# Two expert layers and a linear attention in one program: the iterations that only one stream fills get their router steps, row transposes and key product at other places

## The chip, the cores and the metric

One core of a Trainium2 chip runs the whole program. TensorE (PE) multiplies into PSUM, VectorE (DVE), ScalarE (ACT) and GpSimd (POOL) do the element-wise work, and SyncE (SP) issues most of the DMAs. Each engine works its own instruction list in order and waits on semaphores. The metric is the device time of one execution in microseconds; lower is better.

## The reference

For x of 32 sequences of 256 tokens with 128 channels:

```
x = x + 0.5 * ffn(layernorm(x), router, w1, w2)
x = x + attn(layernorm(x), W_qkv, W_out)
x = x + 0.5 * ffn(layernorm(x), router, w1, w2)

ffn:  probs = sigmoid(x @ router.T)            # 8 experts
      topw, sel = top_k(probs, 2);  topw = topw / (topw.sum + 1e-20)
      h = square(relu(x @ W1[e]))              # expert widths 4 x 128, 4 x 256
      out = sum over e of combine[e] * (h @ W2[e])
attn: q, k, v = x @ W_qkv, 16 heads of 8;  rope on q and k
      qf = elu(q * scale) + 1;  kf = elu(k) + 1
      out = (qf @ (kf.T @ v)) / max(qf . sum(kf), 1e-6);  out @ W_out
```

Every token goes through all eight experts and is weighted by its combine weight, which is zero for six of them. All of it is float32.

## The kernel before, in words

**Groups and streams.** The tokens are worked in NG = 16 groups of 512 tokens. Each group passes three stages: the first expert layer (stream f1), the attention (at), the second expert layer (f2). A software pipeline of 25 iterations (t from -3 to 21) runs f1, at and f2 of different groups side by side; f2 runs SHIFT = 5 groups behind f1. So only f1 has expert work in the first full iterations (t = -1 to 3) and only f2 in the last ones: these are the lone iterations, for which `alone(s, t)` holds.

**Chunks and places.** An expert layer is NC = 12 chunks of 128 hidden columns. An iteration has 24 places; where both streams run there is a chunk at each place, f1's in the first 12, f2's in the next 12; in a lone iteration the chunks stand at every second place. f2's twelve lone chunks begin at place 12 and end in the next iteration. One chunk is: three matmuls up (`up`, lines 509 to 511, the float32 product split in three fp32r products), relu times the gate on VectorE into `hid` (`weighted`, line 1047), the square and the rounded copy `h_hi` on ScalarE (`squares`, lines 740 and 751: the copy of a chunk is issued after the square of the next one of its group), the remainder `h_lo` on GpSimd (`remainders`, line 880), and nine places later three matmuls down (`down`, lines 529 to 531). `hid` has six slots and the up product two PSUM banks.

**The router and the gates.** For the group one iteration ahead: normalise (`norm`), transpose on TensorE (`transpose`, line 471), copy to `xT`, router product (`logits`, line 490), exp and 1 + exp on ScalarE (lines 718 and 722), then on VectorE `take_sigmoid` (972), `best_two` (981), `where_two` (990 to 995), `weigh_two` (1003 and 1007, gives cwt), `choose_two` (1015); on GpSimd `root_of_weights` (874, the square root of cwt, since the gate is applied before the square); on VectorE `spread_roots` (pick at 1025, g_tok at 1031). `weight_rows` transposes g_tok on TensorE (480), `rows_of_weights` copies the rows to SBUF on ScalarE (730), and SyncE writes them to DRAM (395) and broadcasts them to all 128 partitions in four DMAs of 512 KB and less (`g_all`, 407). Chunk 0 of the next group cannot be weighted before its piece of g_all has landed, and a piece is only overwritten when the group before has used it.

**What sets the order.** Each engine has one hand-written function `iteration(t, par)`; the place of a call in it is the place of the work in that engine's queue. TensorE writes transposes and logits into one PSUM bank (`tp`), and `tp_free` holds the order of its five users.

**The start.** w1 is split into `w1_hi` (ScalarE, line 822) and `w1_lo` (VectorE, line 922) in iteration -3, before the first logits; `keep_busy` (line 589) runs idle transposes on TensorE.

## Time and profile before

| | us |
|---|---|
| median of three runs (791.9 to 795.37) | 792.01 |
| the profiled execution | 793.06 |
| its span | 791.3 |

| engine | busy us | share |
|---|---|---|
| TensorE | 729.2 | 92% |
| GpSimd | 686.2 | 87% |
| ScalarE | 597.5 | 76% |
| VectorE | 581.6 | 74% |

Busy time is the sum over an engine's instructions; it doesn't say which engine the others wait for. The matmuls' ends are modelled, so that TensorE's share is no measure of its speed. What an engine waits for stands in the table of waits, and how long one iteration of the pipeline takes is the distance between two first chunks in the timeline. Of the 1.7 us between span and time of the profiled execution the profile shows nothing.

### The profile page before, as it was taken

What the parts mean: (1) busy time and instruction counts of PE and PEld (TensorE: products, weight loads), DVE (VectorE), ACT (ScalarE), POOL (GpSimd) and SP (SyncE); (2) the same over time, 40 slices, a digit from 0 to 9 for tenths busy, and PEclk for the clock granted to TensorE, in tenths of its full rate; (3) what the DMA queues carried; (4) which work ended last, traced back from release to release, by engine and by line L of the source; (5) the groups of instructions that cost most, each with busy time, mean ns of one, the idle gap of its engine ahead of it and who ended that gap; (6) DMA issues with size and microseconds to landing.
All of it is one profiled execution on the core that took longest, in us unless ns stands there. A gap on an engine that the chain in (4) does not pass through costs nothing.

```text
span 791.3 us, 13302 instructions
## 1 busy us (share of the span) xinstructions
PE 729.2 (92%) x3736; PEld 594.3 (75%) x3736; DVE 581.6 (74%) x1832; ACT 597.5 (76%) x1220; POOL 686.2 (87%) x668
## 2 busy tenths in 40 slices
PE   6688788889999999999999999999999998989887
PEld 6466566667888888888888888888887877767665
DVE  3456788877879787877878797878777678676543
ACT  4577677668887978888888879788878766766765
POOL 3778867859999999999999999999999877666876
PEclk9999999989999999999999999999999999999999
DMA  5654113023233222233333332213333403303330
GB/s 181 187 163 133 37 72 107 2 107 108 108 109 121 91 91 69 99 110 108 121 109 120 109 122 84 79 68 112 116 108 121 122 2 107 110 13 121 121 121 27
DMA packets 31160, 79.38 MB, mean 100 GB/s; under 512 B 3312, under 2 KB 14448, under 8 KB 31088
## 3 DMA queue, kind: packets, MB, share of 16 engines
q1 hardware_dynamic: 30800, 78.47, 29.9%
q8 instruction: 30, 0.49, 0.3%
q14 instruction: 42, 0.34, 0.1%
q10 hardware_dynamic: 288, 0.07, 0.0%
HBM read 73.81 MB, written 4.72 MB: 99 GB/s over the span
## 4 chain that ended last, share of the span: by engine, by line
PE 27%; DVE 27%; POOL 18%; issue 13%; ACT 10%; DMA 4%; DVEq 1%; POOLq 0%; ACTq 0%; SPq 0%
POOL h_lo L880 9%; DVE hid L1047 7%; POOL root_f L874 4%; PE bank L509 4%; PE bank L529 3%; PE bank L511 3%; PE bank L510 3%; PE bank L531 3%; PE bank L530 3%; DMA g_all_f<-rows_f 3%; ACT h_hi L751 3%; DVE pick_f L1025 2%; ACT hid L740 2%; POOL x_lo_at L868 2%; ACT xn_f L697 2%
## 5 line engine op out<-in xcount | busy, mean ns | idle before, releaser
L880 POOL TENSOR_TENSOR h_lo<-hid,h_hi 128x512 fp32r<-128x512 f32 x384 | 492.8, 1308 | 70.0 <-ACT h_hi L751 69.4
L1047 DVE SCALAR_TENSOR_TENSOR hid<-bank,g_all_f 128x512 f32<-128x512 f32 x384 | 262.2, 684 | 137.8 <-PE bank L511 90.9
L740 ACT ACTIVATE hid<-hid 128x512 f32<-128x512 f32 x384 | 228.8, 622 | 50.0 <-DVE hid L1047 49.7
L751 ACT ACTIVATE h_hi<-hid 128x512 fp32r<-128x512 f32 x384 | 225.8, 620 | 4.9 <-PE bank L531 0.4
L509 PE MATMUL bank<-x_hi_f,w_hi 128*128 128x512 f32 x384 | 164.3, 428 | 16.1 <-DVE hid L1047 16.1
L529 PE MATMUL bank<-h_hi,w_hi 128*128 128x512 f32 x384 | 154.5, 402 | 12.5 <-POOL h_lo L880 12.5
L531 PE MATMUL bank<-h_hi,w_lo 128*128 128x512 f32 x384 | 152.6, 397 | 0.0
L511 PE MATMUL bank<-x_hi_f,w_lo 128*128 128x512 f32 x384 | 151.9, 396 | 0.0
L530 PE MATMUL bank<-h_lo,w_hi 128*128 128x512 f32 x384 | 151.9, 396 | 0.0
L510 PE MATMUL bank<-x_lo_f,w_hi 128*128 128x512 f32 x384 | 151.5, 395 | 0.0
L509 PEld LDWEIGHTS bank<-x_hi_f,w_hi 128*128 128x128 f32 x384 | 73.1, 190 | 40.7 <-DVE hid L1047 25.2
L529 PEld LDWEIGHTS bank<-h_hi,w_hi 128*128 128x128 f32 x384 | 72.5, 189 | 34.9 <-POOL h_lo L880 20.0
L511 PEld LDWEIGHTS bank<-x_hi_f,w_lo 128*128 128x128 f32 x384 | 72.6, 189 | 17.6
L531 PEld LDWEIGHTS bank<-h_hi,w_lo 128*128 128x128 f32 x384 | 72.4, 188 | 16.6
L530 PEld LDWEIGHTS bank<-h_lo,w_hi 128*128 128x128 f32 x384 | 72.5, 189 | 15.4
L510 PEld LDWEIGHTS bank<-x_lo_f,w_hi 128*128 128x128 f32 x384 | 73.3, 191 | 11.1
L697 ACT ACTIVATE xn_f<-x_sb,nbias_f,rstd_f 128x128 f32<-128x128 f32 x128 | 52.4, 481 | 12.5 <-POOL nbias_f L861 12.5
L874 POOL TENSOR_TENSOR root_f<-cwt_f,c_half 128x8 f32<-128x8 f32 x32 | 54.3, 1697 | 0.0
L868 POOL TENSOR_TENSOR x_lo_f<-xT,x_hi_f 128x512 fp32r<-128x512 f32 x32 | 41.5, 1298 | 12.9 <-DVE x_hi_f L965 12.9
L709 ACT ACTIVATE xT<-bank 128x512 f32<-128x512 f32 x48 | 28.3, 590 | 26.4 <-PE bank L471 16.7
L965 DVE CAST x_hi_f<-xT 128x512 fp32r<-128x512 f32 x32 | 21.6, 676 | 24.3 <-ACT xT L709 24.3
L718 ACT ACTIVATE ex_f<-bank 128x32 f32<-128x32 f32 x32 | 6.3, 197 | 43.0 <-PE bank L490 43.0
(105 smaller groups left out, 1045.2 us busy)
## 6 DMA issues: line engine op xcount, KB each, us to landing
g_all_f<-rows_f SPq DMA_DIRECT2D x128, 512.0 KB, 5.8
x_sb<-in_x SPq DMA_DIRECT2D x16, 256.0 KB, 3.3
out_x<-x_sb SPq DMA_DIRECT2D x16, 256.0 KB, 7.1
g_all_f<-in_w SPq DMA_DIRECT2D x2, 768.0 KB, 6.6
con<-in_const SPq DMA_DIRECT2D x1, 584.0 KB, 6.1
rows_f<-g_row_f SPq DMA_DIRECT2D x32, 16.0 KB, 1.4
g_all_f<-in_wqkv SPq DMA_DIRECT2D x1, 192.0 KB, 6.5
con<-in_const ACTq DMA_DIRECT2D x1, 68.0 KB, 3.2
```

Of the source, the lines that this page charges most:

```text
L509: mm(o, w1_hi[:, w], x_hi[s][u][:], start=True, stop=False)
L510: mm(o, w1_hi[:, w], x_lo[s][u][:], start=False, stop=False)
L511: mm(o, w1_lo[:, w], x_hi[s][u][:], start=False, stop=True).then_inc(s_p1[s], 1)
L529: mm(o, w2_hi[:, c, :], h_hi[:, c, :], start=(c == 0), stop=False)
L530: mm(o, w2_hi[:, c, :], h_lo[:, c, :], start=False, stop=False)
L531: i = mm(o, w2_lo[:, c, :], h_hi[:, c, :], start=False, stop=(c == NC - 1))
L697: i = fn(xn[s][:, k, :], tile, ACT.Identity, bias=nbias[s][:, k:k + 1], scale=rstd[s][:, k:k + 1])
L740: fn(h, h, ACT.Square).then_inc(s_sq[s], 1)
L751: fn(h_hi[:, c, :], hid[:, c % STAGE, :], ACT.Copy).then_inc(s_hhi[s], 1)
L874: gp.tensor_tensor(root[s][:], cwt[s][:], c_half[:], ALU.pow).then_inc(s_root[s], 1)
L880: gp.tensor_tensor(h_lo[:, c, :], hid[:, c % STAGE, :], h_hi[:, c, :].bitcast(F32), ALU.subtract).then_inc(s_hlo[s], 1)
L1047: v.scalar_tensor_tensor(hid[:, c % STAGE, :], hp[c % 2][:], 0.0, g_all[s][:, EXPERT[c], :], ALU.max, ALU.mult).then_inc(s_z[s], 1)
```

## The change

Nothing is computed otherwise and no instruction is added, except in the start: the idle transposes are 27 and 24 where they were 36 and 16. All moves hold in lone iterations alone. In the first stream's, VectorE does `best_two` right after the sigmoid, `where_two` ahead of the fourth chunk, `weigh_two` and `choose_two` behind it and `spread_roots` behind the sixth; GpSimd takes the root one chunk earlier; TensorE transposes the weight rows at place 12 (it was 18), and ScalarE copies them there. In the second stream's, the router steps are drawn together in the same way, the attention's residual sum goes to place 15, TensorE makes keys and values at place 18 (it was 21), rope of the keys goes to places 19 and 20, and in the iteration behind TensorE and ScalarE make the rows at place 3 (it was 6), with `q_features` ahead of `k_features`. The split of w1 goes behind the first gates.

```diff
@@ TensorE
-            keep_busy(a2, 36)
+            keep_busy(a2, 27)
...
                 quarter(t, 0, par)
+                if alone("f2", t - 1):
+                    weight_rows("f2", t + 1 - SHIFT, t)
                 state(t - 2)
                 logits("f1", t + 2)
...
                 if first_time(True, t + 1):
-                    keep_busy(a2, 16)
+                    keep_busy(a2, 24)
                 quarter(t, 1, par)
-                weight_rows("f2", t + 1 - SHIFT, t, 1)
+                if not alone("f2", t - 1):
+                    weight_rows("f2", t + 1 - SHIFT, t)
...
                 if alone("f1", t - 1):
                     back("f1", t)
+                if alone("f1", t):
+                    weight_rows("f1", t + 2, t)
...
                 quarter(t, 5, par)
-                weight_rows("f1", t + 2, t, 4)
+                if not alone("f1", t):
+                    weight_rows("f1", t + 2, t)
+                if alone("f2", t):
+                    kv(t - 1, 0)
+                    kv(t - 1, 1)
                 quarter(t, 6, par)
-                kv(t - 1, 0)
-                kv(t - 1, 1)
+                if not alone("f2", t):
+                    kv(t - 1, 0)
+                    kv(t - 1, 1)
@@ ScalarE
                 exp_logits("f1", t + 2)
+                if first_time(True, t + 2):
+                    act.wait_ge(s_w1, 16)
+                    fn(w1_hi[:], w1_raw, ACT.Copy).then_inc(s_w1hi, 1)
                 squares(t, 0)
+                if alone("f2", t - 1):
+                    rows_of_weights("f2", n2)
...
                 copy_attnT(t - 2)
+                if alone("f1", t):
+                    rows_of_weights("f1", t + 2)
@@ GpSimd
-                remainders(t, 2, 3, 4, 5, 6)
-                root_of_weights("f1", t + 2)
+                remainders(t, 2, 3, 4)
+                if alone("f1", t):
+                    root_of_weights("f1", t + 2)
+                remainders(t, 5, 6)
+                if not alone("f1", t):
+                    root_of_weights("f1", t + 2)
```

`tp_free` now takes the name of the user and puts f1's rows ahead of f2's transpose where f1 is alone. VectorE's moves are shown by its rows. In them `hid` is a chunk's weighting, and f1 and f2 (f10, f20 with a buffer's number) the stream.

VectorE, second full iteration of the first stream (t = 0), from the second chunk's statistics on, before:

```order
L1047 SCALAR_TENSOR_TENSOR hid<-bank1,g_all_f1 128x512
L972 RECIPROCAL prob_f1<-odds_f1 128x32
L957 BN_AGGR mv_f1<-bn_f1 128x2 x4
L981 MAX best_f1<-prob_f1 128x8 x4
L1047 SCALAR_TENSOR_TENSOR hid<-bank2,g_all_f1 128x512
...
L1007 TENSOR_SCALAR cwt_f1,cw_sum_f1<-cw_f1 128x8
L1047 SCALAR_TENSOR_TENSOR hid<-bank2,g_all_f1 128x512
L1015 TENSOR_TENSOR chosen_f1<-which_f1,con 128x64
L1047 SCALAR_TENSOR_TENSOR hid<-bank1,g_all_f1 128x512
L1025 TENSOR_TENSOR pick_f1<-chosen_f1,root_f1 128x64
```

and now:

```order
L1072 SCALAR_TENSOR_TENSOR hid<-bank1,g_all_f1 128x512
L997 RECIPROCAL prob_f1<-odds_f1 128x32
L1006 MAX best_f1<-prob_f1 128x8 x4
...
L1072 SCALAR_TENSOR_TENSOR hid<-bank2,g_all_f1 128x512
L1028 TENSOR_TENSOR cw_f1<-best_f1,rtot_f1 128x8
L1032 TENSOR_SCALAR cwt_f1,cw_sum_f1<-cw_f1 128x8
L1040 TENSOR_TENSOR chosen_f1<-which_f1,con 128x64
L1072 SCALAR_TENSOR_TENSOR hid<-bank1,g_all_f1 128x512
L1072 SCALAR_TENSOR_TENSOR hid<-bank2,g_all_f1 128x512
L1050 TENSOR_TENSOR pick_f1<-chosen_f1,root_f1 128x64
```

The weights (cwt) stand behind the fourth chunk instead of the fifth, and the pick behind the sixth instead of the seventh.

TensorE in the same iteration, from the transpose back of the group before (L542) on, before:

```order
L542 MATMUL bank4<-con,yT 128x128 x4
L509 MATMUL bank1<-x_hi_f11,w1_hi 128x512
...
L509 MATMUL bank2<-x_hi_f11,w1_hi 128x512
...
L531 MATMUL bank3<-h_hi,w2_lo 128x512
L480 MATMUL bank0<-con,g_tok_f1 32x128
L509 MATMUL bank2<-x_hi_f11,w1_hi 128x512
```

and now:

```order
L547 MATMUL bank4<-con,yT 128x128 x4
L485 MATMUL bank0<-con,g_tok_f1 32x128
L514 MATMUL bank1<-x_hi_f11,w1_hi 128x512
L515 MATMUL bank1<-x_lo_f11,w1_hi 128x512
L516 MATMUL bank1<-x_hi_f11,w1_lo 128x512
```

The rows' transpose stands ahead of the up products of chunks 6, 7 and 8 instead of behind them, with three down products between: 18 matmuls in all.

VectorE in a lone iteration of the second stream (t = 18), before:

```order
L981 MAX best_f2<-prob_f2 128x8 x4
L1047 SCALAR_TENSOR_TENSOR hid<-bank2,g_all_f2 128x512
L990 TENSOR_REDUCE tot_f2<-best_f2 128x4
...
L1007 TENSOR_SCALAR cwt_f2,cw_sum_f2<-cw_f2 128x8
L1015 TENSOR_TENSOR chosen_f2<-which_f2,con 128x64
L1047 SCALAR_TENSOR_TENSOR hid<-bank2,g_all_f2 128x512
L1055 TENSOR_TENSOR x_sb<-bank3,x_sb 128x512
L1047 SCALAR_TENSOR_TENSOR hid<-bank1,g_all_f2 128x512
L1025 TENSOR_TENSOR pick_f2<-chosen_f2,root_f2 128x64
```

and now:

```order
L1006 MAX best_f2<-prob_f2 128x8 x4
L1015 TENSOR_REDUCE tot_f2<-best_f2 128x4
...
L1028 TENSOR_TENSOR cw_f2<-best_f2,rtot_f2 128x8
L1072 SCALAR_TENSOR_TENSOR hid<-bank2,g_all_f2 128x512
...
L1040 TENSOR_TENSOR chosen_f2<-which_f2,con 128x64
L1072 SCALAR_TENSOR_TENSOR hid<-bank1,g_all_f2 128x512
L1072 SCALAR_TENSOR_TENSOR hid<-bank2,g_all_f2 128x512
L1050 TENSOR_TENSOR pick_f2<-chosen_f2,root_f2 128x64
L1056 TENSOR_REDUCE g_tok_f2<-pick_f2 128x4x8
L1080 TENSOR_TENSOR x_sb<-bank3,x_sb 128x512
```

The router's steps move ahead of the chunks that stood between them, and the pick ahead of the residual sum and of chunk 6. GpSimd's root of f2 keeps its place, behind chunk 3's remainder.

## Rows read from the trace of the kernel before

**Rows 1.** The waits: engine and line, released by, us in total, times, longest.
```profile
DVE hid L1047 <- DMA g_all_f<-rows_f: 33.8, 10, 7.1
```

**Rows 2.** Busy time by window: length, PE, PEld, DVE, ACT, POOL, granted clock, DMA.
```profile
26.05:49.47 23.42, 19.04 (x79) 13.11 (x79) 12.56 (x42) 16.11 (x32) 19.46 (x18) 1.00 0.51 159
49.47:73.64 24.17, 20.03 (x88) 14.52 (x89) 14.08 (x51) 18.19 (x37) 19.97 (x22) 1.00 0.48 154
718.68:743.85 25.17, 22.14 (x99) 17.24 (x98) 13.65 (x44) 16.91 (x34) 19.01 (x18) 0.93 0.27 97
743.85:766.40 22.55, 19.97 (x89) 15.00 (x88) 13.51 (x35) 14.53 (x28) 19.38 (x16) 1.00 0.32 107
```

**Rows 3.** Timeline of VectorE, first chunks: start, us, line, [idle before, released by].
```profile
49.47 0.69 DVE L1047 SCALAR_TENSOR_TENSOR hid<-bank,g_all_f 128x512 f32<-128x512 f32 x1 [4.12 <-DMA g_all_f<-rows_f]
73.64 0.69 DVE L1047 SCALAR_TENSOR_TENSOR hid<-bank,g_all_f 128x512 f32<-128x512 f32 x1 [4.38 <-DMA g_all_f<-rows_f]
...
658.28 0.69 DVE L1047 SCALAR_TENSOR_TENSOR hid<-bank,g_all_f 128x512 f32<-128x512 f32 x1 [3.54 <-DMA g_all_f<-rows_f]
688.73 0.69 DVE L1047 SCALAR_TENSOR_TENSOR hid<-bank,g_all_f 128x512 f32<-128x512 f32 x1 [2.16 <-DMA g_all_f<-rows_f]
...
766.40 1.29 DVE L1047 SCALAR_TENSOR_TENSOR hid<-bank,g_all_f 128x512 f32<-128x512 f32 x2 [4.45 <-DMA g_all_f<-rows_f]
```

**Rows 4.** Timeline of the start, up to the first router steps.
```profile
4.01 6.13 PE L589 MATMUL bank<-con 128*128 128x128 f32 x36 [4.01 <-DMA con<-in_const]
7.59 1.65 ACT L697 ACTIVATE xn_f<-x_sb,nbias_f,rstd_f 128x128 f32<-128x128 f32 x4 [4.34 <-POOL nbias_f L861]
13.45 0.33 DVE L972 RECIPROCAL prob_f<-odds_f 128x32 f32<-128x32 f32 x1
```

**Rows 5.** Timeline of the iteration from 49.47 us: the gates' way.
```profile
59.14 1.29 POOL L880 TENSOR_TENSOR h_lo<-hid,h_hi 128x512 fp32r<-128x512 f32 x1 [1.34 <-ACT h_hi L751]
60.40 1.63 POOL L874 TENSOR_TENSOR root_f<-cwt_f,c_half 128x8 f32<-128x8 f32 x1
62.06 1.27 DVE L1025 TENSOR_TENSOR pick_f<-chosen_f,root_f 128x64 f32<-128x64 f32 x1 [2.36 <-POOL root_f L874]
64.10 0.27 PE L480 MATMUL bank<-con,g_tok_f 128*32 128x128 f32 x1
67.05 0.34 ACT L730 ACTIVATE g_row_f<-bank,c_cut 32x128 f32<-32x128 f32 x1
67.76 0.34 SPq L395 DMA_DIRECT2D rows_f<-g_row_f  x1
69.31 2.13 SPq L407 DMA_DIRECT2D g_all_f<-rows_f  x4
```

**Rows 6.** Timeline of TensorE there: a down and an up product.
```profile
65.05 0.40 PE L529 MATMUL bank<-h_hi,w_hi 128*128 128x512 f32 x1
65.75 0.39 PE L509 MATMUL bank<-x_hi_f,w_hi 128*128 128x512 f32 x1
```

**Rows 7.** Timeline, second stream: a pick in one iteration, the gates of the next.
```profile
731.73 0.23 DVE L1025 TENSOR_TENSOR pick_f<-chosen_f,root_f 128x64 f32<-128x64 f32 x1 [0.97 <-POOL root_f L874]
...
749.87 0.68 DVE L1047 SCALAR_TENSOR_TENSOR hid<-bank,g_all_f 128x512 f32<-128x512 f32 x1
751.81 1.29 POOL L880 TENSOR_TENSOR h_lo<-hid,h_hi 128x512 fp32r<-128x512 f32 x1 [0.64 <-ACT h_hi L751]
753.07 1.63 POOL L874 TENSOR_TENSOR root_f<-cwt_f,c_half 128x8 f32<-128x8 f32 x1
754.73 1.28 DVE L1025 TENSOR_TENSOR pick_f<-chosen_f,root_f 128x64 f32<-128x64 f32 x1 [1.60 <-POOL root_f L874]
759.74 0.34 ACT L730 ACTIVATE g_row_f<-bank,c_cut 32x128 f32<-32x128 f32 x1
```

**Rows 8.** Busy time by window, columns as in rows 2: two gaps of TensorE.
```profile
83.00:92.00 9.00, 5.53 (x25) 4.10 (x24) 5.63 (x10) 4.97 (x10) 7.96 (x7) 1.00 0.01 2
152.00:164.00 12.00, 8.41 (x36) 6.46 (x35) 11.54 (x49) 6.00 (x12) 8.35 (x11) 0.86 0.34 132
```

**Rows 9.** Timeline of TensorE: the gap inside the first window.
```profile
88.20 0.50 PE L556 MATMUL bank<-x_hi_at,wq_hi 128*128 128x512 f32 x1 [3.47 <-POOL x_lo_at L868]
```

More of the change, by code:

```diff
@@ L448, in _, with tp_free, transpose @@
             mm = nc.tensor.matmul
-            def tp_free(t, pos):
-                n = [done(m + (pos > k)) for k, m in
-                     enumerate((t + 2, t + 1 - SHIFT, t - 1, t + 2 - SHIFT, t + 2))]
-                if due(n[0]):
-                    pe.wait_ge(s_ex["f1"], value(n[0]))
-                if due(n[1]):
-                    pe.wait_ge(s_gr["f2"], value(n[1]))
-                if due(n[2]):
-                    pe.wait_ge(s_xT["at"], value(n[2]))
-                if due(n[3]):
-                    pe.wait_ge(s_ex["f2"], value(n[3]))
-                if due(n[4]):
-                    pe.wait_ge(s_gr["f1"], value(n[4]))
-            def transpose(s, n, t, pos):
+            def tp_free(t, user):
+                if alone("f1", t):
+                    order = ("f1", "f2 rows", "at", "f1 rows", "f2")
+                else:
+                    order = ("f1", "f2 rows", "at", "f2", "f1 rows")
+                pos = order.index(user)
+                group = {"f1": t + 2, "f2 rows": t + 1 - SHIFT, "at": t - 1, "f2": t + 2 - SHIFT, "f1 rows": t + 2}
+                n = {q: done(group[q] + (order.index(q) < pos)) for q in order}
+                if due(n["f1"]):
+                    pe.wait_ge(s_ex["f1"], value(n["f1"]))
+                if due(n["f2 rows"]):
+                    pe.wait_ge(s_gr["f2"], value(n["f2 rows"]))
+                if due(n["at"]):
+                    pe.wait_ge(s_xT["at"], value(n["at"]))
+                if due(n["f2"]):
+                    pe.wait_ge(s_ex["f2"], value(n["f2"]))
+                if due(n["f1 rows"]):
+                    pe.wait_ge(s_gr["f1"], value(n["f1 rows"]))
+            def transpose(s, n, t):
                 if not live(n):
@@ L478, in weight_rows @@
                 pe.wait_ge(s_gt[s], value(n + 1))
-                tp_free(t, pos)
+                tp_free(t, s + " rows")
                 nc.tensor.transpose(tp[0:EXP * TG, 0:P], g_tok[s][:].rearrange("p e k -> p (e k)"), ident) \
@@ L1158, in iteration @@
                     add_moe("f2", t - 1 - SHIFT)
-                k_features(t - 2)
-                q_features(t - 2)
+                if alone("f2", t - 1):
+                    q_features(t - 2)
+                    k_features(t - 2)
+                else:
+                    k_features(t - 2)
+                    q_features(t - 2)
                 weighted(t, 0)
                 high_part("f1", n1, par)
-                spread_roots("f2", n2_last, 0)
+                if not alone("f2", t - 1):
+                    spread_roots("f2", n2_last, 0)
                 weighted(t, 1)
-                spread_roots("f2", n2_last, 1)
+                if not alone("f2", t - 1):
+                    spread_roots("f2", n2_last, 1)
                 weighted(t, 2)
@@ L1189, in iteration @@
                 weighted(t, 10)
+                if alone("f1", t):
+                    spread_roots("f1", n1, 0)
+                    spread_roots("f1", n1, 1)
+                    if first_time(True, t + 2):
+                        split_w1()
                 high_part("at", t - 1, 0)
-                choose_two("f1", n1)
+                if not alone("f1", t):
+                    choose_two("f1", n1)
                 weighted(t, 11)
@@ L1209, in iteration @@
                 mean_variance("at", t)
[L1210 to L1213 removed]
+                if alone("f2", t):
+                    where_two("f2", n2)
+                    weigh_two("f2", n2, 0)
+                else:
+                    best_two("f2", n2)
+                weighted(t, 18)
+                if alone("f2", t):
+                    weigh_two("f2", n2, 1)
+                    choose_two("f2", n2)
+                    stats("f2", t + 3 - SHIFT, 0)
+                else:
+                    add_attention(t - 2)
+                    where_two("f2", n2)
                 weighted(t, 19)
                 rope_q_cos(t - 1)
[L1216 removed]
+                if alone("f2", t):
+                    rope_k(t - 1, 0)
+                else:
+                    weigh_two("f2", n2, 0)
                 weighted(t, 20)
                 rope_q_sum(t - 1)
[L1219 to L1220 removed]
+                if alone("f2", t):
+                    rope_k(t - 1, 1)
+                    rope_k_sum(t - 1)
+                    mean_variance("f2", t + 3 - SHIFT)
+                else:
+                    stats("f2", t + 3 - SHIFT, 0)
+                    weigh_two("f2", n2, 1)
                 weighted(t, 21)
[L1222 to L1224 removed]
+                if not alone("f2", t):
+                    mean_variance("f2", t + 3 - SHIFT)
+                    choose_two("f2", n2)
+                    rope_k(t - 1, 0)
                 weighted(t, 22)
[L1226 removed]
+                if alone("f2", t):
+                    spread_roots("f2", n2, 0)
+                    spread_roots("f2", n2, 1)
+                else:
+                    rope_k(t - 1, 1)
                 weighted(t, 23)
[L1228 removed]
+                if not alone("f2", t):
+                    rope_k_sum(t - 1)
             pipeline(dve, iteration)
```

63 lines of the change are left out of this document (34 added, 29 removed).

## The prediction, made before the changed kernel ran

> **What bounds the kernel now.** I read four views in this order. The table of waits comes first: VectorE stood 33.8 us in all for the gates' broadcast, ten times, once for 7.1 us [rows 1]. That is the most the change can go for: nearly all else it touches has cover. The timeline at the first chunks then says where these waits end something. A first chunk that starts straight behind such a wait sets the distance to the one before: in the first stream at 49.47 and 73.64 (4.12 and 4.38 us idle ahead of it), in the second at 658.28, 688.73 and 766.40 (3.54, 2.16, 4.45) [rows 3]. The busy times between two first chunks give the floor. GpSimd has 19.46 us of work in the 23.42 from 26.05 and 19.97 in the 24.17 from 49.47; in the tail 19.01 of 25.17 and 19.38 of 22.55 [rows 2]. TensorE in the second of them has 20.03, though its gaps are many. So if the gates came at once, a lone iteration would not fall to zero wait: GpSimd would stop it after 20 us, less than 4 us below now, plus whatever GpSimd itself idles. The middle of the program, where both streams run, keeps its order.
>
> Last, the way of the gates in the iteration from 49.47 [rows 5]: the root starts at 60.40, the pick at 62.06, TensorE transposes at 64.10, ScalarE copies the row only at 67.05, SyncE writes it at 67.76, broadcasts at 69.31, and it has landed at 73.64. From row copy to landing is 6.59 us, and nothing in the change shortens that. Between transpose and row copy lie 2.95 us of which the copy needs 0.34: the rest is ScalarE's queue (squares).
>
> **The start.** The 36 idle transposes take 6.13 us from 4.01 and end at 10.14; one is 0.17, so 27 end 1.5 us earlier, at 8.6. The normalised tokens are there at 7.59 + 1.65 = 9.24 [rows 4], so only 10.14 - 9.3, about 0.8, can be won. The split of w1 leaves VectorE's way to the sigmoid at 13.45 too, but the way there is TensorE's and ScalarE's; it is worth nothing more as long as w1's halves are ready for chunk 0, which waits 7.1 us for gates today [rows 1]. The eight more transposes in the next iteration cost 8 x 0.17 = 1.4 us of TensorE inside that wait. I take +0.75 (0 to 1.5).
>
> **First stream, 26.05 and 49.47.** The root moves one remainder (1.3 us) ahead. At 59.14 the remainder ahead of it had itself made GpSimd idle 1.34 us for ScalarE's copy [rows 5], so the root fits nearly into idle time, and g_tok comes about 2 us earlier. The rows' transpose now stands at place 12 instead of 18, ahead of chunks 6, 7 and 8. TensorE is in order, so it stands there until g_tok has come, an estimated 3 to 3.7 us after it is through with chunk 5, because GpSimd, not TensorE, paces those chunks. Behind the transpose it still has to do the products up to the next first chunk: six remaining up triples, the next chunk's one, and six down triples, 13 x 0.70 us (65.05 to 65.75 [rows 6]) = 9.1, plus 0.3 for the transpose and 0.5 for the first product's end: 9.9 us. g_tok is there 11.6 us behind the first chunk by my walk through the queues, so the next first chunk can come after 11.6 + 9.9 = 21.5. The gates would be there after 11.6 + 0.4 + 6.6 = 18.6: the wait for the broadcast goes, and TensorE's queue is late next. Against 23.42 that is +1.9. In the next iteration the GpSimd work is 0.5 us more and it idles while chunk 6 is behind the transpose: a remainder needs the copy that ScalarE issues behind the square of the next chunk, and that chunk is now queued behind the transpose. I put this idle time at 2.8 us, between the 1.34 that it waits at this place now [rows 5] and the 4.2 that would leave no gain: 19.97 + 2.8 = 22.8, against 24.17, +1.4. Bounds for the two together: -1 (GpSimd idle 4.5 us in each) to +6.5 (both at GpSimd's busy time plus 0.8).
>
> **First stream, the three later ones** (from 73.64). They don't end at a gate wait; VectorE has the attention's steps as well. There the moves save a part of VectorE's wait for the root (2.36 us ahead of the pick [rows 5]) and cost TensorE's new wait; I take a third of that wait once, +0.75, bounds -2 and +2.5. The second stream's transpose, which now waits for the row copy on the shared bank, lies in the last of them and is in these bounds.
>
> **Second stream.** Here the root keeps its place, behind chunk 3's remainder, and that remainder waits for ScalarE's copy (0.64 at 751.81 [rows 7]), which waits for chunk 4's square. The router steps (best, the sum, the four finds, reciprocal, weights, choose: about 2 us of short rows) now stand ahead of chunks 3 and 4, so root, today at 753.07, comes 0.8 to 1.7 us later. In exchange the pick is ahead of the residual sum, and the rows leave at place 3, not 6: from pick (754.73) to row copy (759.74) 5.0 us pass [rows 7], of which this can save some 3 where the attention fills the places between. I take +2.0 in the iteration that ends at 658.28 (of 3.54), -0.3 in the next, 0 at 718.68, +0.75 for the one to 743.85, where kv at place 18 gives the state earlier, and -1.3 for the last, where nothing but chunks lies between the places and only the late root is left. Sum +1.15; bounds -2 and +4. Half of the finds' cost would vanish if chunk 4's product is late anyway (TensorE gaps); that is in the bounds.
>
> **Sum.** 0.75 + 1.9 + 1.4 + 0.75 + 1.15 = 5.95, taken as 6.0. The profiled execution took 793.06 (span 791.3 and 1.7 around it), so 787.1; it stands 1.05 above the median of the three runs, 792.01, and against that I forecast 786.0.
>
> **Rivals.**
> *B, TensorE's clock.* In the window from 83 to 92, with a TensorE gap of 3.47 us [rows 9], the granted clock stayed 1.00; over 152 to 164 it was 0.86 [rows 8]. With 2.4 and 1.2 GHz as the levels, 0.86 over 12 us means 3.4 us at the lower one and 1.7 us of work lost. If the new stand at the transpose does this in two iterations in which TensorE's queue is late next, 3.4 us of the head's gain go: 6.0 - 3.4 = 2.6, 789.4. For it: the new gap is about as long as the longest. Against it: rows 8 show such a gap with the clock whole. The Trainium skill (TensorE: Matmul & The Clock Gate, section HAM oscillation) says that pauses of the matmul engine between bursts let its clock drop, so that the next burst starts slow each time; by it every lone iteration with the new stand would pay. This case's trace agrees in the one window and not in the other.
>
> *C, the second stream's late root costs more.* The tail's sum at its lower bound, -2, instead of +1.15: 789.1. For it: the root is behind a remainder that is already waited for (0.64). Against: the waits at 658.28 and 688.73 leave 2 to 3.5 us to win.
>
> *D, the slower side: GpSimd's loop.* Remainders of chunks 5 and 6 are held by the transpose, and GpSimd is the floor. If it idles more than 4.0 us from one first chunk to the next (23.42 - 19.46), the head gets longer. Price: 1.3 us, one remainder, in each of five lone iterations, 6.5, and the last tail term 1.3, less 0.75 from the start and 2.0 at 658.28: 5.0 us slower, 797. Against it: today's idle time at that remainder is 1.34 us [rows 5].
>
> *E, the moves do all they can.* TensorE's stand is under 2 us and the two iterations fall to about 20.5; with the tail at +3 the gain is 10: 782. Against it: 13 triples behind the transpose.
>
> **Chances.** Forecast 0.58 (its own range 783 to 789), B 0.16, C 0.12, D 0.09, E 0.05. What this kernel's measurement can tell from no change is 0.5%, 3.96 us: faster means under 788.05. The forecast's own range lies below that for 0.50 of its 0.58; E and a part of B and C give 0.10 more: faster 0.60. D is slower, 0.09; the rest, 0.31, is no change. The range takes in B and C and most of the forecast: 781.0 to 791.5. Nothing about the middle has to be allowed for.
>
> **What would show it.** Right: the waits for the broadcast fall from 33.8 to about 20; the distances in the first stream read near 21.5 and 22.8; TensorE stands 3 us or more ahead of the first stream's rows' transpose; ScalarE's row copy follows it within 0.5 us; the second stream's root starts 0.8 us or more later behind its first chunk. Wrong: a granted clock below 0.9 in the windows of the first lone iterations (B); GpSimd idle above 4 us there (D); a first chunk at 658.28 that still waits 3 us (C); or a middle part whose length changes, which no step here allows for.

## The result and the profile after

| | before | changed |
|---|---|---|
| median (seven runs each) | 791.9 us | 799.28 us (796.73 to 802.7) |
| profiled execution, its span | 793.06, 791.3 us | 802.7, 800.9 us |
| ratio of the times | | 1.0093, interval 1.0073 to 1.0113 |

The change made the kernel 0.9% slower; 786.0 us, 0.8% faster, had been forecast. The profiled execution of the changed kernel is one of its slower ones, 3.4 us above the median; the comparisons between kernels below go by medians, the traces tell where the time lies.

What the change aimed at, it reached. In the table of waits of the changed kernel (engine and line, released by, us in total, times, longest) the wait for the gates' broadcast is down from 33.8 us [rows 1] to 7.0:

```profile
DVE hid L1072 <- DMA g_all_f<-rows_f: 7.0, 4, 3.4
DVE pick_f L1050 <- POOL root_f L895: 21.3, 9, 3.6
PE bank L485 <- DVE g_tok_f L1056: 17.6, 10, 3.4
...
```

Two other waits grew in its place: VectorE stands for the root (12.4 us over 7 times before, 21.3 over 9 now) and TensorE for the weights that it is to transpose (1.7 us once before, 17.6 over 10 times now). VectorE's waits for a chunk's product rose too, from 90.9 to 104.4 us, and those for a slot that GpSimd has to free from 11.3 to 20.1.

Set beside the windows of before [rows 2], the same stretches of the changed kernel, each from one first chunk to the next (columns: length, PE, PEld, DVE, ACT, POOL, granted clock, DMA):

```profile
24.25:47.93 23.68, 18.65 (x84) 14.23 (x83) 12.58 (x42) 15.70 (x30) 17.04 (x17) 0.93 0.51 183
47.93:72.80 24.87, 20.77 (x90) 15.74 (x88) 14.68 (x51) 17.00 (x34) 19.85 (x22) 0.93 0.45 148
72.80:102.15 29.35, 24.83 (x114) 19.59 (x114) 21.65 (x63) 21.25 (x44) 24.89 (x25) 0.94 0.27 91
102.15:135.85 33.70, 28.81 (x136) 23.29 (x136) 25.75 (x81) 22.27 (x44) 24.35 (x27) 0.90 0.18 64
725.24:749.98 24.74, 21.84 (x99) 17.18 (x98) 14.45 (x44) 16.78 (x35) 18.91 (x19) 0.93 0.20 67
749.98:776.01 26.03, 22.16 (x93) 16.71 (x92) 13.26 (x36) 15.81 (x30) 20.32 (x16) 0.93 0.26 93
```

The third and fourth of before, which the rows above do not have:

```profile
73.64:101.25 27.61, 21.22 (x100) 16.01 (x98) 21.11 (x64) 18.82 (x38) 22.01 (x23) 1.00 0.29 100
101.25:131.73 30.48, 25.88 (x136) 20.62 (x136) 26.32 (x81) 22.03 (x44) 24.37 (x27) 1.00 0.25 83
```

The first chunk comes at 24.25 instead of 26.05 us, so 1.8 us are won in the start. From there on the first four distances read 23.68, 24.87, 29.35 and 33.70 (before: 23.42, 24.17, 27.61 and 30.48), and the last but one 26.03 where it was 22.55. Every one of these windows shows a granted clock under 1.00; the first four of before were at 1.00. GpSimd, which had the most work of the four in the first of them before (19.46 us), is idle for 6.6 of 23.68 us.

The way of the gates in the iteration from 47.93 (timeline: start, us, line, [idle before, released by]) beside [rows 5]:

```profile
58.05 1.64 POOL L895 TENSOR_TENSOR root_f<-cwt_f,c_half 128x8 f32<-128x8 f32 x1
59.72 1.28 DVE L1050 TENSOR_TENSOR pick_f<-chosen_f,root_f 128x64 f32<-128x64 f32 x1 [3.23 <-POOL root_f L895]
61.31 0.39 PE L485 MATMUL bank<-con,g_tok_f 128*32 128x128 f32 x1 [2.80 <-DVE g_tok_f L1056]
61.74 0.36 ACT L745 ACTIVATE g_row_f<-bank,c_cut 32x128 f32<-32x128 f32 x1 [0.62 <-PE bank L485]
...
67.25 2.56 POOL L901 TENSOR_TENSOR h_lo<-hid,h_hi 128x512 fp32r<-128x512 f32 x2 [3.86 <-ACT h_hi L766]
...
72.80 0.69 DVE L1072 SCALAR_TENSOR_TENSOR hid<-bank,g_all_f 128x512 f32<-128x512 f32 x1 [1.22 <-POOL h_lo L901]
```

Root, pick and transpose are at 10.1, 11.8 and 13.4 us behind the first chunk (49.47; before 10.9, 12.6, 14.6), the row copy at 13.8 instead of 17.6. TensorE stood 2.80 us for it, the remainder at 67.25 waited 3.86 us, and the next first chunk waits for no gate: it is released by GpSimd's remainder, through the six slots of `hid`.

The gap's other price, in windows around the stand of the iteration before (TensorE idle from 32.98 to 36.42), columns as above:

```profile
31.00:37.00 6.00, 1.76 (x8) 0.99 (x8) 2.40 (x4) 4.91 (x11) 6.00 (x5) 1.00 0.46 143
37.00:41.00 4.00, 4.00 (x12) 3.14 (x11) 1.38 (x2) 0.92 (x3) 1.50 (x2) 0.57 0.21 77
41.00:47.00 6.00, 6.00 (x30) 4.88 (x29) 2.77 (x4) 5.03 (x9) 4.21 (x4) 1.00 0.58 214
```

and single matmuls of it, in that stretch and behind it:

```profile
38.07 0.63 PE L536 MATMUL bank<-h_hi,w_lo 128*128 128x512 f32 x1
38.49 0.63 PE L514 MATMUL bank<-x_hi_f,w_hi 128*128 128x512 f32 x1
...
41.11 0.39 PE L515 MATMUL bank<-x_lo_f,w_hi 128*128 128x512 f32 x1
41.34 0.39 PE L516 MATMUL bank<-x_hi_f,w_lo 128*128 128x512 f32 x1
```

TensorE has hardly worked up to 36.4, and then runs at the lower of its two levels (1.2 instead of 2.4 GHz, 0.57 in the mean from 37 to 41): a matmul every 0.42 us instead of 0.23, just when six chunks' products are due. That is what the Trainium skill describes for waits on DMAs (TensorE: Matmul & The Clock Gate, section HAM oscillation: the engine waits, and its next burst begins cold, each time round); this trace agrees, with a wait on VectorE.

In the second stream, the iteration from 749.98, beside [rows 7]:

```profile
749.98 0.69 DVE L1072 SCALAR_TENSOR_TENSOR hid<-bank,g_all_f 128x512 f32<-128x512 f32 x1 [1.33 <-DMA g_all_f<-rows_f]
...
757.48 0.07 DVE L1032 DVE_READ_ACCUMULATOR cwt_f<-cw_f 128x1 f32 x1
...
760.04 1.30 POOL L901 TENSOR_TENSOR h_lo<-hid,h_hi 128x512 fp32r<-128x512 f32 x1 [1.94 <-ACT h_hi L766]
761.29 1.64 POOL L895 TENSOR_TENSOR root_f<-cwt_f,c_half 128x8 f32<-128x8 f32 x1
762.89 2.50 POOL L901 TENSOR_TENSOR h_lo<-hid,h_hi 128x512 fp32r<-128x512 f32 x2
762.97 1.27 DVE L1050 TENSOR_TENSOR pick_f<-chosen_f,root_f 128x64 f32<-128x64 f32 x1 [3.59 <-POOL root_f L895]
764.55 0.40 PE L485 MATMUL bank<-con,g_tok_f 128*32 128x128 f32 x1 [2.83 <-DVE g_tok_f L1056]
```

The root stands 11.3 us behind the first chunk; it was 9.2. The weights (cwt) were ready at 757.5. The root was not waiting for them but stood, in GpSimd's order, behind the remainder of chunk 3, and that remainder waited 1.94 us for ScalarE's copy, which comes behind chunk 4's square. VectorE then idled 3.59 us ahead of the pick with chunk 6 behind it.

### The profile page after: what moved, and what is told of

Same layout as the page of the kernel before. It is cut to its first block, busy times and chain, and to the rows that moved or that the text cites. A ratio compares the mean times of both kernels' runs of the same rounds, so it can differ in the third digit from the quotient of the medians.

```text
span 800.9 us, 13300 instructions
## 1 busy us (share of the span) xinstructions
PE 738.6 (92%) x3735; PEld 606.2 (76%) x3735; DVE 585.3 (73%) x1832; ACT 598.3 (75%) x1220; POOL 688.8 (86%) x668
## 4 chain that ended last, share of the span: by engine, by line
PE 34%; DVE 28%; POOL 16%; issue 12%; ACT 8%; DMA 1%; DVEq 1%; POOLq 0%; ACTq 0%; SPq 0%
POOL h_lo L901 8%; DVE hid L1072 7%; PE bank L514 4%; POOL root_f L895 4%; PE bank L516 4%; PE bank L515 4%; PE bank L534 4%; PE bank L536 4%; PE bank L535 4%; PE bank L495 2%; DVE pick_f L1050 2%; ACT h_hi L766 2%; PE bank L610 2%; POOL x_lo_at L889 2%; PE bank L622 2%
## 5 line engine op out<-in xcount | busy, mean ns | idle before, releaser
L1072 DVE SCALAR_TENSOR_TENSOR hid<-bank,g_all_f 128x512 f32<-128x512 f32 x384 | 262.2, 684 | 133.8 <-PE bank L516 104.4
L514 PE MATMUL bank<-x_hi_f,w_hi 128*128 128x512 f32 x384 | 165.4, 431 | 18.0 <-DVE hid L1072 17.6
L516 PE MATMUL bank<-x_hi_f,w_lo 128*128 128x512 f32 x384 | 153.9, 401 | 0.0
```

What stands on the lines that cost most here:

```text
L514: mm(o, w1_hi[:, w], x_hi[s][u][:], start=True, stop=False)
L516: mm(o, w1_lo[:, w], x_hi[s][u][:], start=False, stop=True).then_inc(s_p1[s], 1)
L1072: v.scalar_tensor_tensor(hid[:, c % STAGE, :], hp[c % 2][:], 0.0, g_all[s][:, EXPERT[c], :], ALU.max, ALU.mult).then_inc(s_z[s], 1)
```

## The experiments

Each was timed beside the kernel before on the same chip, and the median of that kernel lay between 791.75 and 792.56 us. "Start" below is the new start (27 and 24 idle transposes, w1 split behind the first gates). Diffs are against the changed kernel, where nothing else is said.

**Does the clock explain it?** Idle transposes fill the stand:

```diff
             def weight_rows(s, n, t):
...
+                tp_free(t, s + " rows")
+                if s == "f1" and alone("f1", t) and not isinstance(t, Step) and t in (-1, 0, 1, 2, 3,):
+                    keep_busy(tp, 12)
+                if s == "f2" and alone("f2", t - 1):
+                    keep_busy(tp, 12)
                 pe.wait_ge(s_gt[s], value(n + 1))
-                tp_free(t, s + " rows")
```

> The changed kernel with 12 idle transposes on TensorE (into the bank of the transposes, which is free by then) ahead of its wait for the weights to be transposed, in every lone iteration of both streams. Clock theory: the changed order lets TensorE stand in each lone iteration, the granted clock then falls to half for a stretch, and nine to ten such stretches of some 3.4 us cost about 1.7 us each. With the gap filled the clock goes back to 0.99 and the kernel to 787 to 791 us. Rival, order theory (remainders and products held behind the weights' transpose): the clock changes but the distances between first chunks do not, 799 us or, with 2 us more work on TensorE in ten iterations, up to 803.

Measured: 796.9 us (ratio 1.0054, 1.0031 to 1.0078), clock 0.991. The clock came back in all but one of the first lone iterations and only some 2.4 us with it. From first chunk to the start of the middle part the head fell from 148.1 to 143.9 us (before: 141.8), the tail from 140.2 to 139.5 (before: 133.0). That lies between the two theories. So the clock is part of the loss in the first stream; in the second, filling the stands gave back next to nothing, though the transposes take TensorE's time there too.

**The parts by themselves.** The kernel before with the start alone; then also the first stream's moves; then the second stream's moves alone. For each, the other stream's `if alone(...)` branches take the old side:

```diff
-                if alone("f2", t):
+                if False:
                     where_two("f2", n2)
```

> The kernel before with the new start alone (27 and 24 idle transposes, w1 split behind the first gates). In the changed kernel the first chunk came at 24.25 us instead of 26.05. Both theories: 1.8 us less, 790.1 us, if the pair of distances behind it stays as before. If the later split of w1 is itself what delays the first iterations, the gain is gone again: 792.

> The changed start and all moves of the first stream, the second stream's as before. The head ended 4.55 us later in the changed kernel (172.37 against 167.82), so 796.5 us if head and tail are independent. Clock theory: half-clock stretches in all the early iterations and at most one or two in the tail.

> The moves of the second stream alone on the kernel before. The changed kernel's part behind 167.82/172.37 us grew by 5.0 us, so 796.9 us; the iteration that ends at the first gate wait of the tail gets about 2.2 us shorter, the five behind it longer by 7. Clock theory: four half-clock stretches between 680 and 770 us, none at 20 to 110. If the late root and not the clock does it, the last iterations are longer with the clock at 1.00.

Measured: start 790.67 (ratio 0.9983, 0.9970 to 0.9995); with the first stream 793.57 (1.0021, 1.0011 to 1.0031); second stream alone 797.04 (1.0061, 1.0039 to 1.0084). The moves of both streams cost: the first stream's 2.9 us on top of the start, the second stream's some 5 us on the kernel before. The first stream came out 3 us below what was expected of it.

**Which move of the first stream?** The rows' transpose and copy at place 18 again, all other moves of the first stream kept, the second stream as before:

```diff
-                if alone("f1", t):
-                    weight_rows("f1", t + 2, t)
...
-                if not alone("f1", t):
-                    weight_rows("f1", t + 2, t)
+                weight_rows("f1", t + 2, t)
```

> The new start and the first stream's moves on VectorE and GpSimd, but the rows' transpose and its copy at place 18 again; the second stream as before. Stand theory (TensorE's stand at place 12 and the clock that it takes): TensorE has no gap of 3.4 and 2.8 us at the rows' transpose, the granted clock is 1.00 from 30 to 150 us, and the time is about 789 to 790.5, 1 to 2.6 below the same moves with place 12 (793.6) and at or under the start alone (790.7). Rival, the moved router steps themselves cost: 793 us as with place 12, without the stand.

Measured: 784.33 us (0.9895, 0.9876 to 0.9914), some 5 us below what even the stand theory expected. The first two distances of this kernel and of the same with place 12, in that order:

```profile
23.86:46.35 22.49, 19.86 (x98) 15.14 (x97) 12.40 (x42) 16.49 (x32) 19.49 (x18) 1.00 0.55 166
46.35:68.19 21.84, 20.00 (x90) 14.22 (x88) 13.93 (x51) 18.24 (x36) 19.70 (x22) 1.00 0.53 170
```

```profile
23.28:47.09 23.81, 18.75 (x85) 14.40 (x84) 12.58 (x43) 15.64 (x30) 17.06 (x17) 0.93 0.58 194
47.09:73.11 26.02, 22.00 (x91) 16.99 (x90) 14.68 (x52) 17.11 (x34) 20.66 (x22) 0.87 0.42 142
```

The router steps drawn together win 6.3 us over the start alone (790.67 to 784.33), and place 12 loses 9.2 of it again, by one edit. With place 18 VectorE still waits for the broadcast (3.59 us ahead of the chunk at 68.19) and is yet 4.2 us faster over that one iteration: the wait for the gates was cheaper than what removed it.

**Which move of the second?** Each with the start and the first stream as before: keys at their old places; rows at place 6 (and features of keys first); only the rows at place 3:

```diff
-                if alone("f2", t):
-                    kv(t - 1, 0)
-                    kv(t - 1, 1)
```

```diff
-                if alone("f2", t - 1):
-                    weight_rows("f2", t + 1 - SHIFT, t)
```

> The new start and the second stream's moves, but keys and values, and rope of the keys, at their old places 21 to 23. If all of the second stream's moves together with the start are worth 796 us (797.0 less 1.1), then: theory that the rope rows in front of chunks 4 and 5 delay VectorE in the iterations that have attention: the iterations from 656 and 688 us get back about 2 and 0.7 us, 793 us. Rival, that the loss is the late root and the rows' stand: unchanged there, 796 us.

> The new start and the second stream's moves, but the rows at place 6 again and the features of keys ahead of those of queries. Stand theory: TensorE's gaps of 2.3 and 2.8 us ahead of the rows' transpose at 734 and 758 us go and the clock with them; the last but one iteration (26.1 us, against 21.9 with the start alone) falls to 23 to 24 and the time to 793. Late-root theory: the root is 2.2 us later in any case, so the gates come no earlier and the iteration stays at 25.5 to 26: 796 us.

> The new start, and of the second stream only the rows at place 3 and q_features ahead of k_features; router steps, residual and keys where they were. Pick and g_tok then stand behind the chunk at place 0, and TensorE may stand for them at place 3. If the 2.15 us won in the iteration from 604 us come from the rows at place 3, it is won here too, and the time is 788.5 to 790; if they come from the router steps drawn together, the iteration stays at 53.9 and the time is 790.7 or above by the stand.

Measured: 795.51 (1.0035, 1.0020 to 1.0050), 796.54 (1.0043, 1.0028 to 1.0059) and 801.96 (1.0115, 1.0096 to 1.0135). Neither of the first two undoes the loss. The third is the worst kernel of all: with the old router steps the pick is still behind the chunk at place 0, and TensorE stands 4.2 us for it:

```profile
677.07 0.68 DVE L1050 TENSOR_TENSOR pick_f<-chosen_f,root_f 128x64 f32<-128x64 f32 x1
```

```profile
678.06 0.28 PE L485 MATMUL bank<-con,g_tok_f 128*32 128x128 f32 x1 [4.21 <-DVE g_tok_f L1056]
```

**The sum of the parts, and the root.** First the changed kernel with place 18 (the edit above); then, on top of it, the root one remainder earlier:

```diff
-                remainders(t, 16, 17, 18)
-                root_of_weights("f2", t + 2 - SHIFT)
+                remainders(t, 16, 17)
+                if alone("f2", t):
+                    root_of_weights("f2", t + 2 - SHIFT)
+                remainders(t, 18)
+                if not alone("f2", t):
+                    root_of_weights("f2", t + 2 - SHIFT)
```

> The changed kernel with one edit undone: the first stream's rows are transposed and copied at place 18 again. Stand theory: place 12 costs the first stream 9.2 us (793.6 against 784.3 with the first stream's moves alone), and head and tail are independent, so 799.3 - 9.2 = 790.1 us. If the clock of head and tail hang together, or the sum of the parts does not hold, the time lies at 793 or above.

> As the run before it, and GpSimd takes the second stream's root ahead of chunk 3's remainder instead of behind it, in lone iterations. Late-root theory: the last but one iteration (26.0 to 26.6 us with the router steps drawn together, 21.9 without) falls to 23 to 24, VectorE's waits ahead of the pick fall from 3.6 to about 2 us, and the time is 3 to 5 us below the run before, 786. Rival, that the stand ahead of the rows is set by something else (the pick's place ahead of chunk 6): within 1 us of the run before.

Measured: 789.08 (0.9955, 0.9940 to 0.9971) and 779.11 (0.9829, 0.9813 to 0.9844). One instruction moved past one other gives 10.0 us, two to three times what was expected. Its last but one iteration, with the first chunk at 730.23:

```profile
737.82 0.08 DVE L1036 DVE_READ_ACCUMULATOR cwt_f<-cw_f 128x1 f32 x1
...
738.38 1.64 POOL L895 TENSOR_TENSOR root_f<-cwt_f,c_half 128x8 f32<-128x8 f32 x1
740.06 0.23 DVE L1054 TENSOR_TENSOR pick_f<-chosen_f,root_f 128x64 f32<-128x64 f32 x1 [0.35 <-POOL root_f L895]
740.38 6.33 POOL L901 TENSOR_TENSOR h_lo<-hid,h_hi 128x512 fp32r<-128x512 f32 x5 [0.35 <-ACT h_hi L766]
741.89 0.27 PE L485 MATMUL bank<-con,g_tok_f 128*32 128x128 f32 x1
```

the distances of this iteration and the one before it:

```profile
707.71:730.23 22.52, 20.57 (x99) 16.05 (x98) 14.48 (x45) 16.72 (x35) 18.88 (x19) 1.00 0.29 88
730.23:751.97 21.74, 20.65 (x94) 15.93 (x92) 12.35 (x36) 15.48 (x30) 20.42 (x16) 1.00 0.31 100
```

and that of the last but one iteration in the run before, with the root late:

```profile
736.95:762.59 25.64, 21.94 (x93) 16.80 (x92) 13.29 (x35) 15.80 (x30) 19.68 (x16) 0.93 0.27 91
```

The root starts 8.2 us behind the first chunk instead of 11.3, in time in which GpSimd had waited for ScalarE anyway. VectorE's wait ahead of the pick shrinks from 3.59 to 0.35 us, the pick from 1.27 to 0.23, since no remainder runs beside it, TensorE doesn't stand at the transpose, the clock is whole, and the distance is 21.74 where it was 25.64 (26.03 in the changed kernel). Of the gain, 7.9 us lie behind the first gate wait of the tail in the two profiled executions (139.0 to 131.2), 1.6 in the iteration ahead of it (51.8 to 50.2).

**Another place for the first stream's rows, and the second stream's router steps alone.** Place 15 (`weight_rows` behind the fifth quarter in all lone iterations but the last, the first stream's moves and the start only); and the first stream with place 18, of the second only the steps drawn together and the residual sum at 15:

```diff
                 quarter(t, 4, par)
+                if alone("f1", t + 1):
+                    weight_rows("f1", t + 2, t)
                 out_proj(t - 2)
```

> The new start and the first stream's moves with the rows' transpose at place 15, between the old 18 and the new 12, where the second stream has no transpose yet; the second stream as before. Stand theory: two more chunks' products are ahead of the transpose, so the stand is under 1 us, no chunk is held, and the gates come up to 1.5 us earlier than with place 18: 782.5 to 784.5. If any place ahead of 18 costs (GpSimd's and VectorE's loop through the products behind it), 787 to 789, halfway to 793.6.

> The first stream's moves with place 18, and of the second stream's only the router steps drawn together with the residual sum at place 15 (rows at place 6, keys and values and their rope at the old places). If those steps carry the second stream's loss (with start and all of the second stream's moves 796, start alone 790.7), it is 788.5 to 790 us against 784.3; if rows at place 3 or keys at 18 carry it, 784 to 786.

Measured: 783.13 (0.9878, 0.9859 to 0.9898) and 794.02 (1.0013, 0.9997 to 1.0029). Place 15 is not told apart from 18 by this pair. The second stream's steps alone cost 9.7 us (784.33 to 794.02), more than expected; rows and keys at their new places gave 4.9 of it back (789.08).

**What place 12 costs, and how much of it is the clock.** The changed kernel with the early root alone; the same with 18, 14 and 8 idle transposes ahead of the first three stands:

```diff
+                tp_free(t, s + " rows")
+                if s == "f1" and not isinstance(t, Step):
+                    keep_busy(tp, {-1: 18, 0: 14, 1: 8}.get(t, 0))
                 pe.wait_ge(s_gt[s], value(n + 1))
-                tp_free(t, s + " rows")
```

> The changed kernel with one edit: in lone iterations GpSimd takes the second stream's root ahead of chunk 3's remainder. The first stream's rows stay at place 12. If head and tail are independent, place 12 costs the same 9.2 us as with the first stream's moves alone: 779.1 + 9.2 = 788.3 us, that is some 11 below the changed kernel. If place 12 is only harmful through the state of the clock that it leaves to the rest, less.

> As the run before it, with 18, 14 and 8 idle transposes (0.17 us each) on TensorE ahead of its wait for the weights in the first three full iterations, which is where its gaps of 3.44, 2.80 and 1.76 us are. The chunks' products stay as late as they are; only the clock is kept. Clock theory: the head gets nearly as short as with place 18, 780 to 782 us. Order theory (the stand itself, with chunks 6 to 8 behind it): the clock is whole and only 1 to 4 us come back, 784.5 to 787.5.

Measured: 788.38 (0.9959, 0.9937 to 0.9980) and 783.53 (0.9891, 0.9858 to 0.9924). Place 12 costs 9.3 us here too (779.11 to 788.38). Its first two distances, without and with the filled gaps:

```profile
23.49:46.19 22.70, 17.63 (x71) 12.49 (x70) 12.48 (x42) 15.23 (x29) 17.01 (x17) 0.92 0.58 197
46.19:71.99 25.80, 21.77 (x91) 16.85 (x90) 14.69 (x52) 17.10 (x34) 20.42 (x22) 0.87 0.43 144
```

```profile
23.91:46.31 22.40, 19.06 (x102) 15.11 (x101) 12.58 (x43) 15.51 (x30) 17.06 (x17) 1.00 0.64 203
46.31:69.66 23.35, 20.70 (x104) 16.12 (x102) 14.69 (x51) 17.00 (x34) 19.85 (x22) 1.00 0.49 158
```

By medians, with the order untouched and the clock at 1.00 in these windows, 4.9 us come back (the profiled execution without the filled gaps is the fastest of its twelve, 785.95 us, so that its windows show less than that). 4.4 remain, and they are, by what is left, the chunks held behind the transpose: 22.40 and 23.35 against 22.15 and 21.80 with place 18, 1.8 us, and 2.9 in the three later lone iterations (95.8 against 92.9). The time lies between what the clock theory and the order theory expected; each is about half of it.

**Do the mends add up?** Early root and place 15; early root and keys at the old places; all three; all three with the second stream's rows back at place 6.

> Early root of the second stream and the first stream's rows at place 15. Place 15 was 1.2 us below place 18 with the second stream as before, within the scatter. If it adds: 778 us. If not: 779.

> Early root, first stream's rows at place 18, and keys and values with their rope at the old places. Theory that rope's rows in front of chunks 4 and 5 cost VectorE: the iteration from 646 us (31.2, against 30.2 with the second stream as before) gets 1 us back, 778. Rival, keys at 18 feed the state earlier and pay for it: 780 to 781.

> Early root, the first stream's rows at place 15, keys and values at the old places. If the parts add: 779.1 - 1.8 (place 15) - 2.8 (keys) = 774.5 us. If both won through the same thing (which iterations fall to the half clock), 776 to 777.

> As the run before it, with the second stream's rows at place 6 and the features of keys first again. With the root late, place 3 won about 5 us (rows and keys together: 789.1 against 794.0). If place 3 is worth 1 to 1.5 us in each of three iterations by itself: 778 us. If it only mended what the late root had spoilt: within 1 us of the run before.

Measured: 777.31 (0.9817, 0.9784 to 0.9849), 776.35 (0.9797, 0.9764 to 0.9829), 773.7 (0.9767, 0.9747 to 0.9787) and 776.99 (0.9821, 0.9794 to 0.9847). Place 15 gives 1.8 and 2.7 us on either base, keys at the old place 2.8 and 3.6; rows at place 3 are worth 3.3. The intervals of single pairs overlap, save for rows at place 3; the two first mends together (779.11 to 773.7) are clear. The kernel with all three is 2.3% faster than before, the best here. One place where keys at 18 cost shows in the timeline of VectorE and TensorE with the early root and keys at 18, and then at 21:

```profile
659.72 1.27 POOL L901 TENSOR_TENSOR h_lo<-hid,h_hi 128x512 fp32r<-128x512 f32 x1 [0.96 <-ACT h_hi L766]
659.75 1.78 DVE L1135 SCALAR_TENSOR_TENSOR ka<-ka,kb 128x512 f32<-128x512 f32 x1
...
662.45 0.50 PE L514 MATMUL bank<-x_hi_f,w_hi 128*128 128x512 f32 x1 [2.28 <-DVE hid L1076]
```

```profile
661.01 0.50 PE L514 MATMUL bank<-x_hi_f,w_hi 128*128 128x512 f32 x1 [0.45 <-DVE hid L1076]
...
662.42 0.69 DVE L1135 SCALAR_TENSOR_TENSOR ka<-ka,kb 128x512 f32<-128x512 f32 x1
```

The sum of rope's halves stood ahead of a chunk's weighting, and took 1.78 us instead of 0.69 beside a remainder of GpSimd; TensorE waited 2.28 us for that chunk. The two iterations with attention took 31.23 and 30.79 us with keys at 18 and 29.59 and 29.28 with keys at 21.

## Why the prediction was wrong, point by point

**The bound.** Right that the gates ended the lone iterations and that GpSimd and TensorE's queue come next: with the gates' waits down to 7.0 us the first two distances are none the shorter. By medians the parts are: gains of 1.1 (start), 6.3 (first stream's steps) and 5.2 us (the second stream's moves once the root is early, 784.33 to 779.11), and losses of 9.2 (place 12) and 10.0 (late root); together 6.6 us slower, where the changed kernel measures 7.4.

**Start.** +0.75 forecast; the time fell by 1.1 us with the start alone, inside its range of 0 to 1.5, but not in the way forecast, so that was luck. The 27 idle transposes took 6.02 us in the changed kernel and not 4.6, and ScalarE's row copy came at 18.25 where it was at 18.33. What came earlier is the landing of the small write of the rows to DRAM, for which SyncE waits ahead of the broadcast (its waits up to 27 us, before and now):

```profile
SPq L397 <- DMA rows_f<-g_row_f: 2.8, 1, 2.8
SPq L397 <- DMA rows_f<-g_row_f: 1.1, 1, 1.1
```

The kernel with the second stream's moves alone, whose start is the old one, waits 3.0 us there; why the write lands sooner with the new start no run shows. With the start alone the first chunk came at 23.57, 2.5 us earlier, and part of that was lost again: the third distance grew from 27.61 to 29.07, with a stretch at the lower clock.

**First stream, place 12.** The step that failed is the one that set the new place against the old kernel and gave it +1.9 and +1.4, and took +0.75 for the three later iterations. The first two distances got 0.3 and 0.7 us longer instead (23.68 against 23.42, 24.87 against 24.17), the three later ones together 5.4 us (99.6 against 94.2). These sizes scatter: the same first-stream code in two other kernels, place 12 with the second stream as before and with the early root, took 49.8 and 48.5 us for the first two (before: 47.6) and 95.1 and 95.0 for the three later ones. With place 18 they are 44.3 and 91.1, so that the later ones, put down to a third of one wait, hold some 4 of the 9.2 us.

Its inner terms held: the 13 triples and what goes with them were put at 9.9 us from transpose to next first chunk, and with the gaps filled they measure 9.97 both times (36.34 to 46.31 and 59.69 to 69.66). Three things were off. The weights were there 12.2 and 13.4 us behind the first chunk and not 11.6. At the lower clock the stretch took 11.5 us instead of 9.97, in both. And the comparison was never made with the other way open to the same router steps: at place 18 the gates land 22.49 and 21.84 us behind the first chunk, though VectorE waits for them. The forecast credited the transpose's new place with the gain of the root and pick. By medians the steps are worth +6.3, place 12 -9.2.

**Rival B, the clock**, was given 0.16 and 3.4 us. It was true in the first stream in every lone iteration but one and is worth 4.9 us there (788.38 to 783.53). The argument against it was one gap of 3.47 us in the old kernel behind which the clock stayed whole [rows 8, 9]; one such row doesn't show that a gap is free. Its sign, a clock below 0.9 in these windows, was set too low: they read 0.93 and 0.93 in the changed kernel and 0.93 and 0.87 with the first stream's moves alone.

**Rival D, GpSimd's loop**, 0.09 and 797 us, names the rest. Its condition, GpSimd idle over 4.0 us from one first chunk to the next, is met in the first two iterations: 23.68 - 17.04 = 6.6 and 24.87 - 19.85 = 5.0; and the chunk that follows is released by GpSimd's remainder. Its price for the five lone iterations, 6.5 us, is near the 6.35 by which they got longer (141.77 to 148.12), but two causes share it: with the clock whole, 4.4 of the 9.3 us that place 12 costs remain. And the remainder is not alone late: with the gaps filled it ends at 46.24 us and TensorE's product for the same chunk at 46.18, so that either would hold the first chunk at 46.31.

**Rival C, the late root**, 0.12 and 789.1 us, had the mechanism of the second stream and too small a price. Its sign didn't show: the chunk at 660.72 doesn't wait for the gates. **Rival E** needed a stand under 2 us; the first two were 3.44 and 2.80.

**Second stream.** +1.15 forecast; measured +4.75 us in the wrong direction (784.33 to 789.08). This is the second step that failed. The delay of the root had been seen and put at 0.8 to 1.7 us; it is 2.1, and what it costs was mis-sized by far: -1.3 in the last iteration was the price in the text, 10.0 us in all is what taking the delay away gives. In the order of the forecast (+2.0, -0.3, 0, +0.75, -1.3) the profiled executions read +2.2, -2.3, -1.8, +0.4 and -3.5 (53.97 to 51.81, 30.45 to 32.77, 29.95 to 31.75, 25.17 to 24.74, 22.55 to 26.03): the first was right, and the loss is not in the last alone. The row that should have warned is the remainder's own wait of 0.64 us ahead of the root [rows 7]: an instruction that already waits passes a delay on, here to VectorE's pick, to chunk 6 behind it, and to TensorE, which stands 2.83 us. Keys at 18 was counted as a gain and is a loss of about 3 us.

**What stays open.** The clock's part in the second stream was not measured by itself. The four distances of the tail read a granted clock of 0.95, 0.95, 0.93 and 0.93 in the changed kernel and 1.00 in all four with the early root, so the clock is in the 10.0 us. Idle transposes ahead of the stands left the tail within 0.7 us, but they take TensorE time too. Nor was it settled why the second stream's steps alone, with rows at 6, cost 9.7 us while rows and keys together give half of it back.

## What to carry to other kernels

Before a step is moved up in an in-order queue to end a wait elsewhere, write down when its input is there and what stands behind it: TensorE standing 3 us for 0.3 us of work cost more than a wait of 4 us on VectorE had. When steps are drawn together on one engine, look at the link on the other engine: the root had to move with its inputs, past one instruction that itself waits. And measure a bundle by its parts: this one held 12.6 us of gain under 19.2 us of loss.

## What the runs showed of the hardware

TensorE's granted clock fell to half behind stands of 2.8 and 3.4 us in an otherwise light stretch, and the matmuls' distance went from 0.23 to 0.42 us; idle transposes in the gap kept it at 1.00. The length of a gap alone doesn't decide. The gap of 3.47 us that left the clock whole in the kernel before [rows 8, 9] is there again in the kernel with the new start alone, and the window behind it is not whole:

```profile
85.47 0.50 PE L561 MATMUL bank<-x_hi_at,wq_hi 128*128 128x512 f32 x1 [3.47 <-POOL x_lo_at L889]
```

```profile
85.00:92.00 7.00, 6.53 (x22) 5.12 (x23) 5.90 (x17) 3.34 (x7) 6.00 (x8) 0.76 0.01 2
```

Another pair says the same: TensorE stands 2.27 and 2.28 us for a chunk at 677.47 and 710.01 in the changed kernel, and 2.28 and 2.30 at 662.45 and 693.44 with the early root; the clock of these iterations is 0.95 in the first and 1.00 in the second.

The pick takes 0.23 us, or 1.27 when it starts beside a remainder of GpSimd, and the sum of rope's halves 0.69 or 1.78. In these rows both engines read two operands in SBUF, GpSimd's instruction began first (762.89 and 762.97, 659.72 and 659.75), and VectorE's ends only behind it: the pick at 764.24 (of the two remainders in the 2.50 us from 762.89 the first is over at an estimated 764.1), the sum at 661.53, where the remainder ends at 660.99. The Trainium skill (SBUF — State Buffer, section SBUF: two separate sides) calls this an exclusive lock on a shared port; the rows agree.
